# Delta turns whose triangular systems are solved by two 64-wide blocks and a corner, and channel-mix means taken one column block later

## What is computed

```python
def step(carry, inp):
    fH, sH, ns = carry
    k_t, v_t, q_t, i_t, nu_t, p_t = inp
    ...
    kv = k_t[:, :, None] * v_t[:, None, :]
    d_fast = kv - k_t[:, :, None] * jnp.einsum('bk,bkv->bv', k_t, fH)[:, None, :]
    fH = fast_alpha * fH + (1 - fast_alpha) * d_fast
    u_slow = (i_t > IMP_TH).astype(x.dtype)
    d_slow = kv - k_t[:, :, None] * jnp.einsum('bk,bkv->bv', k_t, sH)[:, None, :]
    sH = slow_alpha * sH + (1 - slow_alpha) * u_slow[:, :, None] * d_slow
    ...
    o = p_t[:, 0:1] * jnp.einsum('bk,bkv->bv', q_t, fH) + p_t[:, 1:2] * jnp.einsum('bk,bkv->bv', q_t, sH) + p_t[:, 2:3] * ns
...
# channel mix of layer 1
xn = _layernorm(x, g2, b2)
kk = xn @ W_cm
kk = kk * cmk4 + xp4 * (1.0 - cmk4)
rr = jax.nn.sigmoid(xn * cmr + xp * (1.0 - cmr))
vv = jnp.square(jax.nn.relu(kk)) @ W_cp
x = x + rr * vv
```

## Time and profile before

| | us |
|---|---|
| median of 3 runs | 1981.37 |
| lowest, highest | 1979.56, 1985.12 |
| the profiled execution's own time | 1982.84 |
| its span | 1981.0 |

### The profile page before, as it was taken

One profiled execution on the slowest core, in us unless ns is written; L12 is line 12 of the kernel. 1 busy time (PEld: TensorE's weight loads), 2 busy tenths in 40 slices (PEclk: granted clock), 3 DMA queues, 4 the chain that ended last, 5 costly groups with the idle time before them and its releaser, 6 DMA issues. The chain is left out here.

```text
span 1981.0 us, 31299 instructions
## 1 busy us (share of the span) xinstructions
PE 1830.8 (92%) x10880; PEld 1564.9 (79%) x10880; DVE 1468.3 (74%) x2959; ACT 1113.4 (56%) x1997; POOL 307.7 (16%) x282
## 2 busy tenths in 40 slices
PE   7999999997399999999687969999999999999999
PEld 5688888886399999999465647776788888888887
DVE  7567888887477766767689988787776776776675
ACT  3656666664244444343599876664565465466454
POOL 0000002235433223233101011111000000000000
PEclk9999999996699999999799979999999999999999
DMA  3099543359435334322444572333333243142241
GB/s 112 29 378 407 180 161 124 103 117 223 148 65 120 86 86 96 64 44 39 117 106 88 126 210 87 149 117 118 117 139 128 67 167 128 64 170 106 65 170 65
DMA packets 107985, 251.78 MB, mean 127 GB/s; under 512 B 8992, under 2 KB 51616, under 8 KB 99616
## 3 DMA queue, kind: packets, MB, share of 16 engines
q1 hardware_dynamic: 82288, 201.16, 28.6%
q0 software_dynamic: 23680, 46.28, 12.8%
q10 hardware_dynamic: 1888, 2.67, 0.4%
HBM read 172.88 MB, written 107.61 MB: 142 GB/s over the span
## 5 line engine op out<-in xcount | busy, mean ns | idle before, releaser
L1566 POOL DMA_INDIRECT tokens_behind_spare_rows<-yg,row_of_token x70 | 120.2, 1717 | 300.1 <-DVE row_of_token L1729 272.4
L1661 ACT ACTIVATE h<-bank,b1s 128x256 f32<-128x256 f32 x280 | 125.3, 472 | 37.7 <-PE bank L1489 23.4
L1650 ACT ACTIVATE yg<-yt,own_gates 128x256 f32<-128x256 f32 x68 | 31.0, 502 | 191.1 <-DVE yt L1724 184.7
L3244 ACT ACTIVATE hidden_quarter<-hidden_quarter,scl 128x512 f32<-128x512 f32 x96 | 67.6, 721 | 118.9 <-DVE hidden_quarter L3080 118.3
L1238 PE MATMUL bank<-st,L 128*128 128x128 f32 x768 | 117.1, 279 | 13.3 <-DVE st L588 13.2
L972 ACT ACTIVATE L<-bank 128x512 f32<-128x512 f32 x128 | 75.1, 593 | 93.8 <-PE bank L1230 93.5
L2465 PE MATMUL bank<-split_0h,hidden_weights 128*128 128x512 f32 x320 | 126.5, 395 | 0.0
L2465 PE MATMUL bank<-split_1h,hidden_weights 128*128 128x512 f32 x320 | 125.4, 392 | 0.1
L2466 PE MATMUL bank<-split_0l,hidden_weights 128*128 128x512 f32 x320 | 125.3, 391 | 0.0
L2466 PE MATMUL bank<-split_1l,hidden_weights 128*128 128x512 f32 x320 | 125.3, 391 | 0.0
L1230 PE MATMUL bank<-L 128*128 128x128 f32 x640 | 119.0, 276 | 0.0
(11 more groups left out here) (493 smaller groups left out, 6088.3 us busy)
## 6 DMA issues: line engine op xcount, KB each, us to landing
hidden_weights<-hidden_weight_blocks SPq DMA_DIRECT2D x64, 1024.0 KB, 4.8
z_by_expert<-zero SPq DMA_DIRECT2D x64, 520.0 KB, 15.9
hidden_weight_blocks<-in_ffn_dram SPq DMA_DIRECT2D x14, 1024.0 KB, 13.2
ckb<-in_ffn_dram POOLq DMA_DIRECT2D x32, 352.0 KB, 5.5
xg<-z_by_expert SPq DMA_DIRECT2D x36, 260.0 KB, 3.4
x_tok<-in_w_dram SPq DMA_DIRECT2D x8, 1024.0 KB, 7.9
x_tok<-x_T SPq DMA_DIRECT2D x16, 512.0 KB, 6.0
x_tok<-after_time_mix SPq DMA_DIRECT2D x15, 512.0 KB, 8.2
```

The lines of the kernel that those rows point to most:

```text
L1566: pool.indirect_dma_start(x2_d, bass.IndirectOffsetOnAxis(to_row[:, j:j + 1].bitcast(u32), 0), yg[:, j, :], None, compute_op=ALU.add).then ...
L1661: nc.scalar.activation(h32[:, m, :], B[m % 4][:, 0:TT], ACT.Gelu_apprx_tanh, bias=b1s[:, e * KH + m:e * KH + m + 1]).then_inc(h_act, 1)
L3244: A_.activation(QB[to][:, m, :], src, ACT.Gelu, scale=scl[:, off[lay.name] + row:off[lay.name] + row + 1]).then_inc(g_act, 1)
```

## The change

**Delta turns.** Each 128 x 128 system is split into its two diagonal blocks of 64 (rows and columns 0 to 63, and 64 to 127) and the corner between them. `masks` now writes the two diagonal blocks, plain and transposed, with two instructions of 64 partitions, and the corner with a third. `level` squares both blocks in levels 0 to 4, the first block on partitions 0 to 63 and the second on 64 to 127, into the same PSUM bank. In levels 1 to 5 it multiplies the powers with the inverse made so far (`inverse`), not with X; level 0 has no product, and DVE forms the first inverse as identity less block (`twin`). In level 6 PE multiplies corner and inverse (L1270 of the new file, copied by ACT's new `corner_products`) and applies the inverse to X (L1276), in level 7 it applies the corner (L1279), which DVE subtracts from the lower half. ACT's `square` now copies 256 columns, not 512, and in n = 1 waits for DVE's first inverse too.

**Channel mix.** `mean` of a block is no longer issued at the end of a round but after the first column (m = 0) of the next.

```diff
@@ masks, apply (DVE)
-                for m in range(2):
-                    gm = B[bk][:, m * 128:(m + 1) * 128].rearrange("p (o n) -> p o n", o=1)
-                    V.tensor_tensor(L[:, p, j, 0, 2 * m:2 * m + 2, :], gm.broadcast_to([128, 2, 128]),
-                                    maskL[:, m, :, :], ALU.mult)
+                gram = B[bk][:, 0:256].rearrange("p (m o n) -> p m o n", m=2, o=1)
+                for h in range(2):
+                    V.tensor_tensor(pair(p, j, 0)[half[h]], gram[half[h], :, :, half[h]].broadcast_to([DS, 2, 2, DS]),
+                                    maskL[half[h], :, :, half[h]], ALU.mult)
+                V.tensor_tensor(corner(p, j)[half[1]], gram[half[1], :, 0, half[0]], maskL[half[1], :, 0, half[0]], ALU.mult)
...
-                    V.tensor_tensor(z_ if SQUARES <= n < LEVELS - 1 else x_, x_, B[2 + j][:, 0:256],
-                                    ALU.subtract if n == 0 else ALU.add).then_inc(ap_rdy, 1)
+                        V.tensor_tensor(inv, twin, pair(p, j, 0)[:, :, 1, :], ALU.subtract).then_inc(ap_rdy, 1)
+                        continue
...
+                    if n <= SQUARES:
+                        V.tensor_tensor(inv, inv, B[2 + j][:, 0:128].rearrange("p (m n) -> p m n", m=2),
+                                        ALU.add).then_inc(ap_rdy, 1)
+                    elif n < LEVELS - 1:
+                        V.tensor_copy(x_, B[2 + j][:, 0:256]).then_inc(ap_rdy, 1)
+                    else:
+                        V.tensor_tensor(x_[half[1]], x_[half[1]], B[2 + j][half[1], 0:256], ALU.subtract).then_inc(ap_rdy, 1)
@@ ACT
+            def corner_products(t, p):
+                for j in range(2):
+                    act.wait_ge(sq_ps, t * (2 * SQUARES + 2) + (2 * SQUARES + j + 1))
+                    A_.activation(corner_inverse(p, j)[half[0]], B[j][half[0], 0:128].rearrange("p (m n) -> p m n", m=2),
+                                  ACT.Copy).then_inc(sq_cp, 1)
...
                 at(u, 1, 5, columns, 0)
+                if deltas:
+                    corner_products(t, p)
                 if head:
                     right_side(t + 1, 1 - p, 0)
@@ level (PE)
+                                for h in half:
+                                    T.matmul(B[j][h, 128 * m + 64:128 * m + 128], ab[h, m, 0, :], ab[h, m, 1, :], start=True, stop=True)
+                            for h in half:
+                                last = T.matmul(B[j][h, 128 * m:128 * m + 64], ab[h, m, 1, :], ab[h, m, 0, :], start=True, stop=True)
                         last.then_inc(sq_ps, 1)
...
+                    if n <= SQUARES:
+                        for m in range(2):
+                            for h in half:
+                                last = T.matmul(B[2 + j][h, 64 * m:64 * m + 64], ab[h, m, 0, :], inv[h, m, :], start=True, stop=True)
+                    elif n < LEVELS - 1:
+                        for m in range(2):
+                            last = T.matmul(B[j][half[0], 64 * m:64 * m + 64], corner(p, j)[half[1], m, :], inv[half[1], m, :],
+                                            start=True, stop=True)
+                        last.then_inc(sq_ps, 1)
+                        pe.wait_ge(x_rdy, t * 2 + (j + 1))
+                        for m in range(2):
+                            for h in half:
+                                last = T.matmul(out[h, :, m, :], inv[h, m, :], X[h, p, j, :, m, :], start=True, stop=True)
+                    else:
+                        for m in range(2):
+                            last = T.matmul(out[half[1], :, m, :], corner_inverse(p, j)[half[0], m, :], X[half[0], p, j, :, m, :],
+                                            start=True, stop=True)
@@ channel mix (PE)
                     last.then_inc(cm_ps, 1)
+                    if b >= 1 and m == 0:
+                        mean(b + 1)
...
+                    elif i == 0:
+                        mean(NB + 1)
                     if b >= 1:
                         down(b - 1, i)
-                    if i == 3 and b < NB:
-                        mean(b + 2)
```

More of the change, by code:

```diff
@@ L193, in build @@
         QM = sb("QM", [128, 2, 2, 2, 128], to=pa)
+        Lp = L[:, :, :, :, :, :].rearrange("p b j s a n -> p b j s (a n)")
+        pair = lambda p, j, s_: Lp[:, p, j, s_, 0:256].rearrange("p (m f n) -> p m f n", m=2, f=2)
+        inverse = lambda p, j: Lp[:, p, j, 0, 256:384].rearrange("p (m n) -> p m n", m=2)
+        corner = lambda p, j: Lp[:, p, j, 0, 384:512].rearrange("p (m n) -> p m n", m=2)
+        corner_inverse = lambda p, j: Lp[:, p, j, 1, 256:384].rearrange("p (m n) -> p m n", m=2)
+        twin = Z[:, 1, 0, :, :]
         YT = sb("YT", [128, 2, 128], to=pa)
@@ L566, in _ @@
             dve.sem_inc(pp_rdy, 1)
+            for h in range(2):
+                for m in range(2):
+                    go(V.tensor_copy(twin[half[h], m, :], ident[half[h], half[h]]))
             def masks(t, p, j, bk=4):
@@ L1215, in grams, with level @@
                          start=True, stop=True).then_inc(g_ps, 1)
-            def level(t, p, n, first):
+            def level(t, p, n):
                 for j in range(2):
@@ L1225, in level @@
+                    ab, inv = pair(p, j, n % 2), inverse(p, j)
+                    out = B[2 + j][:, 0:256].rearrange("p (a m d) -> p a m d", a=2, m=2)
                     if n < SQUARES:
                         for m in range(2):
-                            a, b_ = Ln[:, 2 * m, :], Ln[:, 2 * m + 1, :]
                             if n < SQUARES - 1:
-                                T.matmul(B[j][:, 256 * m:256 * m + 128], b_, a, start=True, stop=True)
-                            last = T.matmul(B[j][:, 256 * m + 128:256 * m + 256], a, b_, start=True, stop=True)
+                                for h in half:
+                                    T.matmul(B[j][h, 128 * m + 64:128 * m + 128], ab[h, m, 0, :], ab[h, m, 1, :], start=True, stop=True)
+                            for h in half:
+                                last = T.matmul(B[j][h, 128 * m:128 * m + 64], ab[h, m, 1, :], ab[h, m, 0, :], start=True, stop=True)
@@ L1231, in level @@
                         last.then_inc(sq_ps, 1)
-                    if n > 0:
-                        pe.wait_ge(ap_rdy, t * (2 * LEVELS) + (2 * (n - 1) + j + 1))
-                    elif not first:
-                        pe.wait_ge(ap_rdy, t * (2 * LEVELS) + (j - 1))
-                    for m in range(2):
-                        right = X[:, p, j, :, m, :] if n <= SQUARES else Z[:, j, :, m, :]
-                        last = T.matmul(B[2 + j][:, 0:256].rearrange("p (a m d) -> p a m d", a=2, m=2)[:, :, m, :],
-                                        Ln[:, 2 * m + 1, :], right, start=True, stop=True)
+                    if n == 0:
+                        continue
@@ new lines, in level @@
+                    pe.wait_ge(ap_rdy, t * (2 * LEVELS) + (2 * (n - 1) + j + 1))
+                    if n <= SQUARES:
[12 more added lines that the diff above has]
+                    else:
+                        for m in range(2):
+                            last = T.matmul(out[half[1], :, m, :], corner_inverse(p, j)[half[0], m, :], X[half[0], p, j, :, m, :],
+                                            start=True, stop=True)
@@ L1342, in turn @@
                     if deltas:
-                        level(t, p, n, not tail)
+                        level(t, p, n)
                     if tail:
```

26 lines of the change are left out of this document (15 added, 11 removed).

## The result

| | before | changed |
|---|---|---|
| median us (9 runs each) | 1981.62 | 1964.05 |
| lowest, highest | 1977.98, 2355.88 | 1960.72, 1973.77 |
| span of the profiled execution | 1981.0 | 1959.0 |

A forecast was written before the change was run, and what follows sets the result against it. PE was taken to bound the turns, DVE close behind in late ones. From the profiled 1982.8 us, 37.5 less for turns and 4 for channel mix gave 1941.3, median 1.5 below: 1940; own range 1915 to 1962, with rivals to 2010.

The forecast's parts named there:

- What bounds the turns: Delta turns: PE sets the pace, DVE close behind in late ones; PE's work per turn falls from 22.5 to 18.3 us.
- about 6.6: Delta turns: us of PE's work per turn outside the 68 level products, which take 15.0 us.
- The small products: Levels of a turn: 64-row halves run side by side at 0.055 us a product, 8.4 us a turn, about 0.2 a switch.
- The first rival: Small products' halves run one behind the other, 0.11 us apart, 15.4 us a turn on PE: 2006 us, chance 0.22.
- ACT and DVE: Delta turns: square copies fall to about 0.38 us, DVE additions to 0.28; DVE ends at some 18.1 us in a late turn.
- third rival: Halves side by side, but corner chain and DVE hold late turns; only early turns gain: 1960 to 1975 us, chance 0.12.
- The path through a turn: Stretches between DVE's marks: late pairs of turns 4.28 us less, early turns 3.3 each; 40 over 16 turns, 37.5 counted.
- The second rival: Turns: PE's instructions or clock limit; half of the turns at 1.2 GHz is +7 us a turn, over 2050, chance 0.08.
- Its other half: The second rival's instruction limit: a turn has some 512 PE instructions and loads of level products instead of 272.
- POOL's chain: Behind the turns: hidden sums and scatters with DMA waits of 6.03 and 7.93 us, to 518.58, only shift.
- The sums at 440.09: POOL's hidden sums, taken to start after 15 of 16 turns; its first sums were to start near 402.
- Channel mix: Moved mean: six products ahead of it shorten each of three PE waits by 1.3 us; -4 us, bounds -8 to +8.

The follow-up runs named there:

- `halves_in_turn`: Changed kernel with the small products of all first halves issued before those of the second halves, not in alternation: 1996.42 us, ratio 1.0089 to before.
- `fill2`: Changed kernel plus two unread 128 x 128 x 256 products a turn ahead of the transposes of Y: 1948.67 us, ratio 0.9830 to before.
- `before_thin`: Kernel before with squares of levels 1 to 3 multiplying only 64 of 128 moving columns, all 128 rows kept: ratio 1.0043 to before.
- `mean_only`: Kernel before with only the channel mix's mean moved behind the first column of the next round: 1978.48 us, ratio 0.9984.
- `before_thin64`: Kernel before with squares of levels 1 to 3 using 64 columns of weights and 64 moving columns, all 128 rows kept: ratio 1.0019.
- `delta_only`: Changed kernel with the channel mix's mean back at the end of the round: 1974.02 us, ratio 0.9951 to before.
- `scatters_late`: Changed kernel with all POOL scatters but the last block's issued behind the turns and hidden sums: 2013.63 us, ratio 1.0104 to before.
- `before_slow_dve`: Kernel before with two extra sums over 512 columns in DVE's program of each turn, ahead of the outputs: ratio 1.0052 to before.

## Why the prediction missed

- **What bounds the turns.** PE, as read in the earlier trace rows: shorter products made shorter turns. Its work in a late turn came down to 17.3 to 18.4 us, 18.3 were forecast (the "about 6.6" of other work is 7.5 by the numbers beside it, and the sum used 7.5). But its 1.1 us of pauses a turn were taken to stay small, and no step asked what they would be once its work fell below DVE's.
- **The small products.** Right: 0.058 us side by side against 0.055, and 0.35 a pair of switches against 0.41. The first rival (one behind the other, chance 0.22) did not come: two tiles of 64 rows write different partitions of one bank at 0.058 a product, where products of one tile start 0.117 apart (`halves_in_turn`). The rule in the Trainium skill, TensorEngine Tiling (Array Packing), section Restrictions and Gotchas, that different row tiles cannot access the same bank simultaneously, does not hold as a price here: by it the products would start 0.11 apart, the trace has 0.058. (The two tiles here differ in their columns of the array as well as in their rows.)
- **ACT and DVE.** Right in size for the single instruction (378 and 283 ns). DVE's sum was too low: 18.1 us in a late turn were forecast, it has 18.8 and 19.3. The measured time lies in the third rival's 1960 to 1975, but not for its reason: the corner's copy is waited for nowhere, and the late turns gain as much as forecast where the clock is not slow.
- **The path through a turn.** At 2.4 GHz the forecast holds: 2.1 us less in a late turn were forecast, those without slow clock have 1.6 to 2.9. For 13 of the 15 turns some run with the changed turns has one at 2.4 GHz without gaps; the shortest of each add up to 265.4 us, the same 13 took 297.8 before. That is 2.5 us a turn, as are 37.5 over 15. From `fill2`, 44.4 us less of slow clock took 12.6 us off the 15 turns, filler included, 0.28 us each; the 23.9 us that it still has above before would give 6.7 more, and 316.8 - 6.7 = 310, where 346.9 - 37.5 = 309.4 was forecast. The 310 is an estimate; no run had all turns at 2.4 GHz.
- **The failed step.** The second rival: "The changed turns hold less work and more pauses of PE, so it may fall there", chance 0.08 and priced at half of all turns, over 2050. It was no rival of the forecast but a term of it, and the sum had it at nothing: 68 us more at 1.2 GHz, which cost the 20 us between 37.5 and 17.5. The earlier trace rows showed such falls behind a pause; the sum took the clock at 1.00 because it was 1.00 in turns whose pauses were short. The forecast's own range, which ended at 1962, had no such term either. The rival's price was wrong too: it let each us of PE's work at 1.2 GHz cost as much again, half of all turns and over 2050, while the 68 us cost about 0.3 each, it seems because part of them fell into time in which PE would have waited.
- **Its other half**, a limit of PE's instructions, may be what came on other occasions: gaps of 0.4 us from the first scatter on, with which the 15 turns took 342.1 us instead of 329.4 and the ratio was 0.9962 to 0.9989 instead of 0.9919. The trace of before has no such gap, and on one of these occasions the late turns of `before_thin` took as long as before. So the failure of the sum does not need them: the first runs had all but none.
- **POOL's chain.** The turns' gain went on to the scatters in full, and its waits for the sums' DMAs shrank from 6.03 and 7.93 us to 5.35 and 5.80: 2 us more. The sums at 440.09, taken for the first, are the second of four groups (the first start at 415.8, now 398.0); they came at 423.5, not near 402.
- **Channel mix.** Right: 5 us by the last variance, 4 forecast. The gated network, with 4 us more of slow clock, gave 2 back. `mean_only` gives 3.2 by its ratio.

## What to carry to other kernels

Where PE's work in a loop is cut below that of its neighbours, the loop does not only stop getting shorter: the pauses that open can lower PE's clock, and part of the gain is paid back as PE at 1.2 GHz. Ask of each cut how long PE will then stand still and in which place, and try a product that nobody reads in the longest pause. Here 0.86 us of it a turn took the ratio from 0.9919 to 0.9830, some 15 us, in the runs without gaps; with the gaps it went from 0.9989 to 0.9963 and the turns did not get shorter. So such a kernel is to be timed on more than one occasion beside the kernel before.

## What the hardware showed that was not expected

- A float32 product with 128 columns of weights takes 0.22 us with 64 moving columns as with 128; with 64 columns of weights and 64 moving ones, 0.117 (`before_thin`, `before_thin64`). Halving only the moving side buys nothing.
- Trains of eight instructions for one tile of 64 rows overlap those for the other only from 0.29 us on (`halves_in_turn`), alternation from the first.
- The same turns had 72 or 85 us of slow clock in two kernels (changed, `delta_only`), and the same kernel had 0.6 or 7.6 us of gaps in PE for "issue" on different occasions. In `scatters_late`, with POOL's scatters behind the turns, the gaps were gone.
- Two more sums of 0.68 us on DVE in every turn, an engine busy for 19.4 of 24.0 us, did not lengthen the late turns of 24.3 us at all (`before_slow_dve`).
